# Small weights sent between the first x loads; left halves of a chunk loaded once the copy two chunks back is made; packed weights by parity

## What is computed

```python
def reference(x, ...):
    act = _ln_c(x)                                       # eps 1e-6, no weights
    a = ln(act, ln_in_w, ln_in_b)
    left  = m * (a @ left_proj_w.T + left_proj_b)   * sigmoid(a @ left_gate_w.T + left_gate_b)
    right = m * (a @ right_proj_w.T + right_proj_b) * sigmoid(a @ right_gate_w.T + right_gate_b)
    t = einsum('bikc,bjkc->bijc', left, right)           # one 256x256x256 product per channel
    t = ln(t, ln_c_w, ln_c_b)
    x = x + (t @ out_proj_w.T + out_proj_b) * sigmoid(a @ gating_w.T + gating_b)
    n = ln(x)                                            # no weights
    p = softmax(n @ router_w + router_b); top_p, top_i = top_k(p, 2); top_p /= sum(top_p)
    y = einsum('nd,edc->nec', n, expert_w) + expert_b    # 8 experts
    return x + (the two chosen experts' y, weighted by top_p)
```

## Time and profile before

| | us |
|---|---|
| runs | 1148.45, 1157.99, 1147.43 (median 1148.45) |
| the profiled execution | 1146.6 |
| its span, first to last instruction | 1144.8 |
| mean granted TensorE clock | 0.96 |

### The profile page before, as it was taken

One profiled execution on the slowest core, in us unless ns is written; L12 is line 12 of the kernel. 1 busy time (PEld: TensorE's weight loads), 2 busy tenths in 40 slices (PEclk: granted clock), 3 DMA queues, 4 the chain that ended last, 5 costly groups with the idle time before them and its releaser, 6 DMA issues.

```text
span 1144.8 us, 18926 instructions
## 1 busy us (share of the span) xinstructions
PE 1028.2 (90%) x5658; PEld 560.0 (49%) x5658; DVE 876.6 (77%) x3030; ACT 641.7 (56%) x1134; POOL 748.6 (65%) x727
## 2 busy tenths in 40 slices
PE   1688889987789469999999999999999999999997
PEld 0466666776678243444444444444444444444432
DVE  2899999921111668988888898889888888988883
ACT  0355556611111137676677767676766767676754
POOL 5778788322121338787777878787877878787843
PEclk9899999988899669999999999999999999999999
DMA  7188777958963110111111111111111111111000
GB/s 198 49 286 266 267 285 240 356 196 238 285 191 112 37 29 28 56 38 56 48 46 56 38 56 38 56 38 56 40 55 50 44 56 38 56 38 56 28 29 37
DMA packets 98904, 119.38 MB, mean 104 GB/s; under 512 B 6390, under 2 KB 72182, under 8 KB 96758
## 3 DMA queue, kind: packets, MB, share of 16 engines
q1 hardware_dynamic: 97138, 117.74, 32.2%
q10 hardware_dynamic: 1668, 0.46, 0.2%
HBM read 67.33 MB, written 50.33 MB: 103 GB/s over the span
## 4 chain that ended last, share of the span: by engine, by line
PE 58%; ACT 14%; DVE 13%; issue 8%; DMA 2%; ACTq 1%; POOL 1%; SPq 1%; DVEq 0%; POOLq 0%
PE b_m L794 15%; PE ring L780 7%; PE ein L693 7%; PE b_d L741 7%; DVE stage L871 6%; ACT x2d L560 5%; PE pr_a L655 4%; DVE bst L858 4%; PE b_g L724 4%; PE b_g L718 3%; ACT ttn L543 3%; PE b_g L731 3%; PE b_t L718 3%; PE b_m L788 2%; ACT sig_c L550 2%
## 5 line engine op out<-in xcount | busy, mean ns | idle before, releaser
L442 POOL TENSOR_TENSOR zb<-bcs,x2d 128x512 f32<-128x512 f32 x224 | 286.3, 1278 | 181.9 <-ACT bcs L576 179.6
L794 PE MATMUL b_m<-zb,w_exp 128*64 128x512 f32 x1024 | 278.1, 622 | 0.2
L1034 DVE TENSOR_TENSOR zb<-ring,x2d 128x512 f32<-128x512 f32 x288 | 197.8, 687 | 75.6 <-PE ring L780 75.0
L576 ACT ACTIVATE bcs<-ring 128x512 f32<-128x512 f32 x224 | 133.9, 598 | 168.7 <-PE ring L780 168.3
L560 ACT ACTIVATE x2d<-x2t 64x512 f32<-64x512 f32 x256 | 160.6, 627 | 3.5
L655 PE MATMUL pr_a<-w_proj,xts 64*128 64x256 f32 x1024 | 139.7, 402 | 23.6 <-DVE stage L871 22.9
L871 DVE SCALAR_TENSOR_TENSOR stage<-pr_a,mt,sig_a 128x128 f32<-128x128 f32 x512 | 147.9, 418 | 10.3 <-ACT sig_a L507 10.3
L780 PE MATMUL ring<-wt,sel 32*128 32x512 f32 x512 | 128.6, 498 | 3.1 <-DVE zb L1034 2.3
L780 PEld LDWEIGHTS ring<-wt,sel 32*128 32x128 f32 x512 | 47.6, 183 | 170.7 <-DVE zb L1034 81.5
L507 ACT ACTIVATE sig_a<-pr_a 128x512 f32<-128x512 f32 x128 | 76.5, 597 | 81.7 <-PE pr_a L655 81.6
L655 PEld LDWEIGHTS pr_a<-w_proj,xts 64*128 64x128 f32 x1024 | 96.1, 191 | 52.9 <-issue 32.3
(11 more groups left out here) (132 smaller groups left out, 1834.0 us busy)
## 6 DMA issues: line engine op xcount, KB each, us to landing
left_right_scratch<-stage SPq DMA_DIRECT2D x16, 2048.0 KB, 7.5
chunk<-left_right_scratch SPq DMA_DIRECT2D x24, 1024.0 KB, 9.1
xc<-in_x SPq DMA_DIRECT2D x64, 256.0 KB, 2.8
out<-outc SPq DMA_DIRECT2D x64, 256.0 KB, 2.0
chunk<-left_right_scratch SPq DMA_DIRECT2D x12, 384.0 KB, 7.5
chunk<-left_right_scratch SPq DMA_DIRECT2D x8, 192.0 KB, 5.4
chunk<-left_right_scratch SPq DMA_DIRECT2D x4, 256.0 KB, 7.9
chunk<-left_right_scratch SPq DMA_DIRECT2D x8, 64.0 KB, 4.7
```

The costliest lines, as they stand in the source:

```text
L442: pool.tensor_tensor(zb[:, m % NZ, :], bcs[:, tiles_before(POOL_TILES, ku, ku, m) % 2, :], x2d[:, ku % 2, m % 2, :], ALU.mult)\
L576: act.activation(bcs[:, tiles_before(POOL_TILES, ku, ku, m) % 2, :], ring[:, bcast_bank(ku % 2, m), :], ACT.Copy).then_inc(bcast_out, 1)
L794: ins = pe.matmul(b_m[t * C:(t + 1) * C, :], w_exp[:, ep, :], zb[:, (2 * ep + t) % NZ, :], start=False, stop=ep == EP - 1, skip_group_chec ...
L1034: dve.tensor_tensor(zb[:, m % NZ, :], ring[:, bcast_bank(ku % 2, m), :], x2d[:, ku % 2, m % 2, :], ALU.mult)\
```

## The change

It has four parts.

1. Setup. The 10 small weights leave ACT's queue and are issued by SP between the first and the second x transfer. On DVE the folding comes before the statistics of rows 16 to 31, and the four copies into `w_og` come after stage A. On POOL the first two pieces are scaled one after the other (product, sum, product, sum).
2. Stage B. The two left parts of chunk c are issued as soon as `pack_left` of chunk c - 2 is done; the two right parts still wait for PE.
3. Stage C. `sel` gets a second copy, one for each parity of the unit, with zeros where the other parity's weights lie; the tokens are packed in another order, so that each half of the tokens holds 64 neighbouring partitions with both parities. A `bcast` matmul now contracts over 64 partitions in place of 32, `bias` over 128 in place of 64. `bias_hi`, `bias_lo` and `eb_wide` are twice as wide.
4. POOL makes `sel` by one small and two large operations in place of two small and one large; the copy of the logits on DVE (L1061) and one small operation (L943) write in the new order.

```diff
-            load_x(0)
+            load_x(0, [0])
+            for col, name in enumerate(["ln_in_w", "ln_in_b", "ln_c_w", "ln_c_b"]):
+                sp.dma_start(ln_col[:, col:col + 1], twice(weights[name].rearrange("(c a) -> c a", a=1))).then_inc(w_in, 16)
+            for k, name in enumerate(PROJ):
+                sp.dma_start(bias_row[:, k * C:(k + 1) * C],
+                             weights[name + "_b"].rearrange("(a c) -> a c", a=1)).then_inc(w_in, 16)
+            load_x(0, [1])
             load_x(1)
...
             for c in range(2, CHUNKS):
+                sp.wait_ge(packed, c - 1)
+                load_blocks(c, c % 2, slice(0, BLOCKS), range(0, 2 * Q, 2))
                 sp.wait_ge(ein_ready, (c - 1) * CHUNK)
-                load_blocks(c, c % 2, slice(0, BLOCKS))
+                load_blocks(c, c % 2, slice(0, BLOCKS), range(1, 2 * Q, 2))
...
-            norm_a(0, (0, 1))
+            norm_a(0, (0,))
+            norm_a(0, (1,))
...
-                rows = slice(ku % 2 * 2 * ROUTE + m % 2 * ROUTE, ku % 2 * 2 * ROUTE + m % 2 * ROUTE + ROUTE)
-                pe.matmul(ring[:, bcast_bank(ku % 2, m), :], sel[rows, m // 2 * 2:m // 2 * 2 + 2, :].rearrange("p e c -> p (e c)"),
+                rows = slice(m % 2 * 2 * ROUTE, (m % 2 + 1) * 2 * ROUTE)
+                pe.matmul(ring[:, bcast_bank(ku % 2, m), :], sel[rows, ku % 2, m // 2 * 2:m // 2 * 2 + 2, :].rearrange("p e c -> p (e c)"),
                           wt[rows, ku // 2 % 2, :], start=True, stop=True).then_inc(bcast_ready, 1)
...
-                rows = slice(ku % 2 * 2 * ROUTE, (ku % 2 + 1) * 2 * ROUTE)
                 for part, b in enumerate((bias_hi, bias_lo)):
-                    pe.matmul(b_m[:, :], b[rows, :], wt[rows, ku // 2 % 2, :], start=part == 0, stop=False, skip_group_check=True)
+                    pe.matmul(b_m[:, :], b[:, ku % 2, :], wt[:, ku // 2 % 2, :], start=part == 0, stop=False, skip_group_check=True)
```

More of the change, by code:

```diff
@@ L124, in metaformer_kernel @@
         w_og = keep("w_og", [P, 2, C])
-        bias_hi = keep("bias_hi", [P, P], F32R)
-        bias_lo = keep("bias_lo", [P, P], F32R)
+        bias_hi = keep("bias_hi", [P, 2, P], F32R)
+        bias_lo = keep("bias_lo", [P, 2, P], F32R)
         router_bias = keep("router_bias", [P, E])
@@ L239, in _, with load_x @@
         def _(sp):
-            def load_x(s):
-                for h in range(2):
+            def load_x(s, halves=range(2)):
+                for h in halves:
                     if s >= 2:
@@ L468, in _ @@
             pool.wait_ge(sel_made, 1)
-            pool.tensor_tensor(kind[:, 0:2, :], kind[:, 0:2, :], kind[:, 2:4, :], ALU.add).then_inc(sel_made, 1)
-            pool.wait_ge(sel_made, 2)
-            ins = pool.tensor_tensor(sel[:, :, :], kind[:, 0, :].unsqueeze(2).broadcast_to([P, E, C]),
-                                     kind[:, 1, :].unsqueeze(2).broadcast_to([P, E, C]), ALU.add)
+            for w in range(2):
+                ins = pool.tensor_tensor(sel[:, w, :, :], kind[:, w, :].unsqueeze(2).broadcast_to([P, E, C]),
+                                         kind[:, 2 + w, :].unsqueeze(2).broadcast_to([P, E, C]), ALU.add)
             ins.then_inc(sel_made, 1)
@@ L876, in _ @@
             bn(0, range(ROWS))
-            bn(0, range(ROWS, SUPER))
             in5, out1 = slice(0, 5 * C), slice(5 * C, 6 * C)
@@ L887, in _ @@
                .then_inc(set_dve, 1)
+            bn(0, range(ROWS, SUPER))
             dve.wait_ge(pool_const, 4)
@@ L890, in _ @@
             dve.tensor_tensor(w_proj[:, :], w_proj[:, :], ps_set[:, 4, 0:6 * C], ALU.add).then_inc(set_dve, 1)
-            dve.wait_ge(set_dve, 2)
-            for w in range(2):
-                for half in range(2):
-                    part = slice(half * C, half * C + C)
-                    dve.tensor_copy(w_og[part, w, :], w_proj[part, (4 + w) * C:(5 + w) * C])
             dve.wait_ge(set_act, 1)
@@ L903, in _ @@
                         bn(s + 2, range(k * SUPER // of, (k + 1) * SUPER // of))
+            dve.wait_ge(set_dve, 2)
+            for w in range(2):
+                for half in range(2):
+                    part = slice(half * C, half * C + C)
+                    dve.tensor_copy(w_og[part, w, :], w_proj[part, (4 + w) * C:(5 + w) * C])
             dve.wait_ge(set_pe, 4)
```

31 lines of the change are left out of this document (13 added, 18 removed).

## The result

| | before | after |
|---|---|---|
| runs, us | 1148.45, 1157.99, 1147.43 | 1097.87, 1100.26, 1100.15 |
| median | 1148.45 | 1100.15 |
| span of the profiled execution | 1144.8 | 1096.1 |
| mean granted clock in it | 0.96 | 0.975 |

The ratio after to before is 0.955, with a 95% interval of 0.947 to 0.963. The forecast was 1101.

A forecast was written before the change was run, and what follows sets the result against it. Bounds: late setup and stage A start, stage B's PE waits for POOL's copy behind chunk DMA, PE's own order in stage C. 15 + 26 + 6.5 = 47.5 off 1146.6 gave 1099 profiled, 1101 against the median; range 1092 to 1116.

The forecast's parts named there:

- Setup and stage A, -15: Setup and stage A: earlier small weights and reordered DVE and POOL work start stage A's second super at 55.1, saving 15 us.
- the cover named: Setup: POOL's piece 0, ready at 20.4, was to cover PE, itself ready by 17 to 20 us.
- the step that POOL takes back what DVE wins: Stage A: DVE's first product comes 15 to 18 us earlier, but POOL's piece 2, ready at 35.2, holds pair 6 until 37.7.
- The 0.7 us that the step added for pair 14: Stage A: POOL's piece 4, ready at 49.1, puts pair 14 at 51.6, where DVE would want it at 50.9.
- Its fear for the copies' new place: End of stage A: if the four `w_og` copies meet a busy POOL, they cost at most 4 us.
- Stage B, -26: Stage B: loading left halves early removes 17.8 us of PE idleness and some 8 of slow records, 26 us.
- the 0.8 us that the step had to spare: Stage B: right half's load and copy take 13.0 us while PE has 13.8 us of work on the other chunk.
- Stage C, -6.5: Stage C: `bias` in the turns' 128-row shape saves 0.20 us in each of 32 even units, nothing in odd ones.
- `bias` gains in every unit: Rival, stage C: ACT too finds slack, so odd units gain as well, 1095 us; chance 0.06.
- Late loads in stage B: Rival: stage B's loads still come late, 14 us gained there instead of 26, 1113 us; chance 0.12.
- The taller `bcast` tiles: Rival, stage C: taller `bcast` tiles no longer run side by side, 0.33 us more a pair, +84, 1185 us; chance 0.04.
- The setup's half: Rival: the setup gains half, as small transfers hold x back or the mask lands late, 1108 us; chance 0.07.

The follow-up runs named there:

- t_onepart: The changed kernel with only one of a chunk's two left parts loaded early in stage B, three parts waiting for PE: 1111.40 us.
- t_packearly: The changed kernel with a semaphore of its own for left parts, so POOL packs a left half without waiting for the right half: 1097.29 us.
- s_gate: The changed kernel with ACT's `gate` (sig_c) moved ahead of its second `double` in odd units of stage C: 1088.28 us.
- s_gate_old: The changed kernel with part 3 undone, and ACT's `gate` moved ahead of its second `double` in odd units: 1107.88 us.
- t_bcast32: The changed kernel with each `bcast` multiplying only the 32 rows of its own unit, `bias` staying on 128 rows: 1101.47 us.
- t_wog: The changed kernel with only the four `w_og` copies put back into the setup, ahead of the statistics of super 1: 1100.86 us.

## Why the prediction was right, and where its steps were off

**Setup and stage A, -15: measured -14.6.** PE's first matmul came at 11.85, not at 9 to 11: the step that took a small transfer's issue for cheap was off, since four of them took 1.5 to 1.8 us. It cost 0.6 us at most: the cover named, POOL's piece 0, was ready at 20.68, and the first turn came at 21.27, once DVE's add was done. That add stood behind statistics that waited until 17.53 for the second x transfer, which SP issued behind the small weights. First turn 21.27 (20 to 21 forecast), first product 28.04 (25 to 28), pair 6 at 38.25 (37.7), second super at 55.65 (55.1): the step that POOL takes back what DVE wins is what the rows show, with DVE idle for 3.16 us ahead of pair 6. The 0.7 us that the step added for pair 14 are right by luck: piece 4 was ready at 49.5 and pair 14 did not wait, while DVE waited 0.53 us ahead of pair 8, where PE's records ran at a granted clock of 0.50 (38 to 40 us) after its wait for piece 2. The fourth x transfer let DVE wait 0.45 us and no more.

What the step left open was what each edit of part 1 is worth. The runs show that it can't be split: 10.2 for the copies (1.1 of it not theirs), 12.1 for the rest, 12.8 for both. Its fear for the copies' new place came to nothing, they take 0.17 to 0.19 us each there.

**Stage B, -26: measured -24.0 in the profile, 21.9 between the medians.** The mechanism is shown twice, by the part undone and by the half measure of `t_onepart`. The term was sized too high by 2 us. It had 9.1 us from the request of the right half to POOL's start; that is what chunks 3 and 5 to 7 show (9.0 to 9.3), but for chunks 2 and 4 it was 10.5, past the 0.8 us that the step had to spare: two gaps of 0.6. Why the two take longer is not settled; that the copy behind the right half is what made them gaps is shown by `t_packearly`. The gaps are 0.75 us each from start to start, chunks 2 and 4, behind them, took 0.1 more than 13.8, and chunk 0 was 0.2 longer than before (15.57 from start to start against 15.37): together 1.9.

**Stage C, -6.5: measured -9.5 from the first to the last `bias`.** The 0.20 us in even units is right to the hundredth. Odd units were put at nothing and gave 0.09, which is the step that was off. Summed up, the even units gave 5.8 us (the last two of them nothing) and the odd ones 3.7. Of the 3.7, 1.2 are the interval of unit 61 alone (11.29 before, 10.06 after), and they are not part 3's, as it is 10.06 with part 3 undone too. So part 3 was worth 8.3 us here as well, 1.8 more than the term. The step took ACT's run from xtn to sig_c as fixed; but a copy of a `bcast` tile in it, which reads what PE gives, stood 2.13 us behind xtn before (799.66 to 801.79) and stands 2.06 behind it now (779.68 to 781.74), and the copy in the middle of the two `double` follows 1.74 us later instead of 1.76. So about half of PE's 0.20 was gained in an odd unit, and the rest is wait: the idle time of PE ahead of `x_turn` rose from 5.4 us to 8.5, 0.10 a unit where 0.2 was forecast. That ACT sets the odd units, on which the split rests, is shown by `s_gate`, and that `bias` would pay there too without it, by `s_gate_old`. "`bias` gains in every unit" was thus the wrong rival for this kernel and the right one for the kernel with `gate` moved.

The rule of the Trainium skill (TensorE: Matmul & The Clock Gate, Part 3, The mechanism), by which the 128-row weight load would have to wait for the turns and the gain be 0.10, is not what the trace shows: 0.19 less from the first turn to `bias_lo`. The same section of the Trainium skill also lets a load into the background weight buffer run ahead of matmuls in flight; that agrees with the turns, which follow each other by 0.11.

**The rivals.** Late loads in stage B: partly true, 2 us of the 12 it held. The taller `bcast` tiles: a pair takes 0.42 to 0.43 us as before, and `t_bcast32` says the same. The setup's half: not seen.

**The sum.** The terms 15, 26 and 6.5 gave 47.5; the stages gave 14.6, 24.0 and 9.5, the fill took 1.0 and the tail gave 1.6. The last two are not the change's: the tail was 11.7 us with part 3 undone as well, and 13.3 in `t_bcast32`, and the fill lay between 55.2 and 57.8 over all kernels. So the terms were off by 0.4, 2 and 3, and two of these cancelled in part: that the forecast of 1101 came within 1 us of 1100.15 is luck to that extent. What the second `sel` costs was not tested by itself; the fill, 57.0 with it and 56.2 with part 3 undone, lies inside the spread of all kernels.

## What to carry to other kernels

When several edits lead to the same wait, price each one alone and with the others in place: here two were worth some 10 and 12 us alone and 13 together. For a buffer that is handed back late, what counts is the transfer that is left at that moment, plus every copy behind it, against the time of the work that covers it; give each half its own semaphore, so that the copy does not wait for data it doesn't read. And when a saving shows in every other unit only, find who sets the rest: one move of an instruction on ACT took 9.5 us off stage C, more than the 8.3 of part 3's new layout.

## What the runs showed of the hardware

A small copy on DVE waits for POOL's whole instruction. In the earlier trace rows the four 64x64 copies take 7.49 us while POOL's products and sums of 1.9 us each run; in `t_wog` they took 192 to 1795 ns, the longest beside a POOL instruction that ran from 22.80 to 24.73; behind stage A, with POOL idle, they took 167 to 192 ns:

```profile
L897 DVE COPY w_og<-w_proj x4: 192/668/1795, 21.6 to 24.8; 64x64 f32<-64x64 f32 x4
```

```profile
L907 DVE COPY w_og<-w_proj x4: 167/189/192, 215.1 to 215.6; 64x64 f32<-64x64 f32 x4
```

The Trainium skill (SBUF — State Buffer, Who interferes with whom) has DVE, in modes that a copy can enter, and POOL share one pair of ports, which whoever starts first holds for its whole instruction; the rows agree.

A matmul that changes the height of PE's tile costs about 0.20 us against one that keeps it, here from the 128-row turns to `bias` on 64 or on 128 rows. For `bcast`, 64 or 32 rows among 128-row neighbours make no difference, and `bias_lo` follows `bias_hi` by 0.33 us on 64 rows and on 128. So it is the change that costs, not the height, as far as these shapes show: no run put `bcast` on 128 rows.

The issue of a small transfer on SP's queue took 0.24 us for the last five and 1.5 to 1.8 for four of the first five. ACT's queue issued beside three of these four, but not beside the slowest (1.80 us at 7.54), so what makes an issue slow stays open.
